# Gate matmuls moved behind the weighted sums, and the context limit to the front of VectorE's list, in a pass-pipelined attention and expert kernel

## The reference

```python
logits = x @ gate_weight.T                       # 8 experts
topk_w, topk_idx = jax.lax.top_k(softmax(logits), 2)
y = routed experts (silu(gate) * up, down) + shared expert
x = x + y
```

## Time and profile before

| What | Value |
|---|---|
| median of three runs | 1449.7 us (1448.55 to 1450.1) |
| the profiled execution | 1446.31 us, its span 1444.6 us |
| mean granted TensorE clock | 0.98 |
| TensorE busy | 1340.1 us, 93% of the span |
| VectorE, ScalarE, GpSimd busy | 61%, 47%, 26% |
| chain that ended last, by engine | TensorE 80%, VectorE 11%, issue 2%, ScalarE 2%, DMA 2% |

### The profile page before, as it was taken

How to read it: one execution, slowest core, us unless ns; L and a number is a source line. 1 busy time by engine, 2 the same in 40 slices (tenths; PEclk the granted TensorE clock), 3 DMA queues, 4 the chain that set the end, 5 groups by cost and what they waited for, 6 DMA issues and landing times.

```text
span 1444.6 us, 34230 instructions
## 1 busy us (share of the span) xinstructions
PE 1340.1 (93%) x11411; PEld 1005.0 (70%) x11412; DVE 884.4 (61%) x1952; ACT 674.4 (47%) x1500; POOL 372.7 (26%) x480
## 2 busy tenths in 40 slices
PE   4799999999999997788999999999999999999997
PEld 4688788888888885656767756666666666657675
DVE  6888888888888888667855532232232232224566
ACT  6276667777676776431444423333333333332121
POOL 4322222222222220004566011111111111104554
PEclk9899999999999998899999999999999999999999
DMA  5556766776767658497734622222222222227996
GB/s 197 134 141 190 198 196 185 204 204 199 189 185 202 185 138 270 129 350 134 113 53 83 148 95 81 80 86 80 81 85 82 80 86 81 81 72 235 315 312 225
DMA packets 212740, 223.20 MB, mean 155 GB/s; under 512 B 84693, under 2 KB 142109, under 8 KB 212334
## 3 DMA queue, kind: packets, MB, share of 16 engines
q1 hardware_dynamic: 193608, 178.62, 43.5%
q0 software_dynamic: 12880, 35.47, 8.1%
q10 hardware_dynamic: 6198, 8.40, 2.0%
HBM read 129.30 MB, written 67.96 MB: 137 GB/s over the span
## 4 chain that ended last, share of the span: by engine, by line
PE 80%; DVE 11%; issue 2%; ACT 2%; DMA 2%; SPq 1%; POOL 0%; DVEq 0%; POOLq 0%; ACTq 0%
PE psum_b L726 44%; PE psum_a L726 30%; PE psum_b L1016 2%; PE psum_b L1038 2%; DVE z_parts L1472 1%; DVE k_scale L1394 1%; DVE d_m L1705 1%; PE psum_b L752 1%; SPq L488 1%; DVE wdn L1791 1%; DMA heads<-in_wk_t 1%; DVE gate_act L1680 1%; ACT z_parts L1120 1%; DMA wgu_in<-base_rows 1%; PE psum_b L784 0%
## 5 line engine op out<-in xcount | busy, mean ns | idle before, releaser
L726 PE MATMUL psum_a<-wgu,zg_t 128*128 x1704 | 267.7, 314 | 2.1 <-DVE zg_t L1802 1.7
L726 PEld LDWEIGHTS psum_a<-wgu,zg_t 128*128 128x128 f16 x1704 | 166.1, 98 | 90.2 <-issue 10.3
L726 PE MATMUL psum_a<-zt_in,wsgu 128*128 128x256 f16 x1536 | 170.6, 273 | 1.0 <-ACT y_sb L1306 0.8
L2025 POOL DMA_INDIRECT zg<-z_rows,gather_ix x71 | 67.2, 946 | 402.9 <-DVE gather_ix L1798 395.8
L726 PEld LDWEIGHTS psum_a<-zt_in,wsgu 128*128 128x128 f16 x1536 | 148.8, 98 | 24.9 <-issue 6.5
L1807 DVE SCALAR_TENSOR_TENSOR silu<-psum_a,w_scale,silu 128x352 f32<-128x352 f32 x71 | 41.5, 584 | 191.1 <-ACT silu L1293 191.1
L726 PE MATMUL psum_b<-wdn,act_t 128*128 (+1 forms) x639 | 149.6, 379 | 1.6 <-DVE act_t L1814 1.6
L726 PE MATMUL psum_b<-wsdn,sh_t 128*128 128x512 f16 (+1 forms) x576 | 134.4, 388 | 14.9 <-DVE sh_t L1686 14.4
L1912 POOL TENSOR_SCALAR var_eps<-mv 128x1 f32<-128x1 f32 x64 | 28.4, 443 | 429.7 <-DVE mv L1371 289.9
L1293 ACT ACTIVATE silu<-psum_a,w_scale 128x352 f32<-128x352 f32 x71 | 39.4, 554 | 202.4 <-PE psum_a L726 202.4
L726 PEld LDWEIGHTS psum_b<-wsdn,sh_t 128*128 128x128 f16 (+1 forms) x576 | 54.6, 99 | 88.9 <-issue 18.3
(11 more groups left out here) (247 smaller groups left out, 2346.8 us busy)
## 6 DMA issues: line engine op xcount, KB each, us to landing
expert_rows<-y_sb SPq DMA_DIRECT2D x71, 256.0 KB, 2.0
k_st<-k_parts SPq DMA_DIRECT2D x192, 64.0 KB, 2.0
q_st<-q_parts SPq DMA_DIRECT2D x180, 64.0 KB, 2.0
wgu_in<-in_wgu_t SPq DMA_DIRECT2D x8, 1408.0 KB, 16.5
x_sb<-in_x SPq DMA_DIRECT2D x16, 512.0 KB, 5.5
cx_in<-in_ctx_t SPq DMA_DIRECT2D x16, 512.0 KB, 8.8
x_res<-in_x SPq DMA_DIRECT2D x16, 512.0 KB, 6.3
value_rows<-heads SPq DMA_DIRECT2D x16, 512.0 KB, 3.3
```

The source lines that it names most:

```text
L726: return nc.tensor.matmul(o, l, r, start=start, stop=stop)
L2025: pool.indirect_dma_start(out=zg[:, b, :], out_offset=None, in_=z_d[:, :], in_offset=bass.IndirectOffsetOnAxis(ap=gather_ix[:, b:b + 1], a ...
```

## The change

The gate matmuls of a pass get a step of their own, R, in bank A0 (that of the first scores), instead of L in B2; only pass 16, outside the loop, keeps L in B2. On TensorE the weighted sums come directly behind turning z, then the gate matmuls, then `turn_bound`, then `turn_logits`, which now also waits until R is drained. ScalarE copies both halves of z ahead of the two high halves. VectorE finds and spreads the context's limit right behind the values, ahead of `z_low` and `logits_out`.

```diff
-ROUTE = [("L", "B2")]
+ROUTE = [("R", "A0")]
+LAST_ROUTE = [("L", "B2")]
...
-FULL_PASS = (AHEAD + SCORES + AHEAD_KQ + OUT + AHEAD_V + BEHIND + ROUTE
-             + [("P0", "A2"), ("P1", "A3")] + TURN_ROUTE + BOUND)
+FULL_PASS = (AHEAD + SCORES + AHEAD_KQ + OUT + AHEAD_V + BEHIND + ROUTE + LAST_ROUTE
+             + [("P0", "A2"), ("P1", "A3")] + BOUND + TURN_ROUTE)
...
+def route_step(i):
+    return "L" if isinstance(i, int) and i == NB else "R"
...
             def route(i):
-                wait_free(pe, "L", i)
+                wait_free(pe, route_step(i), i)
...
             def turn_logits(i):
                 wait_free(pe, "LT", i)
+                settle(pe)
+                wait_drained(pe, route_step(i), i)
                 settle(pe)
...
                 if behind:
                     turn_z(i)
-                if behind:
-                    route(i)
                 attend(0, i)
                 attend(1, i)
                 if behind:
-                    turn_logits(i)
+                    route(i)
                 if ahead:
                     turn_bound(i)
+                if behind:
+                    turn_logits(i)
...
             def z_out(i):
                 turned_out(i, 0)
+                turned_out(i, 1)
                 z_high(i, 0)
-                turned_out(i, 1)
...
                 if ahead:
                     values_out(i)
+                if ahead2:
+                    weigh_context(i + 2)
+                if ahead:
+                    spread_context()
                 if behind:
                     z_low(i, 0)
                     logits_out(i)
                     z_low(i, 1)
-                if ahead2:
-                    weigh_context(i + 2)
-                if ahead:
-                    spread_context()
                 if weighs:
                     weigh_piece(i, weighs)
```

More of the change, by code:

```diff
@@ L86 @@
 IS_BEHIND = {name for name, _ in OUT + BEHIND + ROUTE + TURN_ROUTE}
+ONLY_LAST = {name for name, _ in LAST_ROUTE}
 def steps_of(i):
     names = [name for name, _ in FULL_PASS]
+    if i == NB:
+        return [n for n in names if n in IS_BEHIND - {"R"} | ONLY_LAST]
+    names = [name for name in names if name not in ONLY_LAST]
     if i < 0:
         return [n for n in names if n in IS_AHEAD]
-    if i == NB:
-        return [n for n in names if n in IS_BEHIND]
     return [n for n in names if not (i == 0 and n in IS_BEHIND) and not (i == NB - 1 and n in IS_AHEAD)]
@@ L105, in earlier_fills @@
         return whole + sum(n in mine for n in names[:names.index(step)])
-    return (i - 1) * len(mine) + earlier_fills(step, 1)
+    return (i - 1) * len(mine - ONLY_LAST) + earlier_fills(step, 1)
+def route_step(i):
+    return "L" if isinstance(i, int) and i == NB else "R"
 class Chain:
@@ L787, in route @@
             def route(i):
-                wait_free(pe, "L", i)
+                wait_free(pe, route_step(i), i)
                 pe.wait_ge(z_turned, i * SUB)
                 for kc in range(KC):
-                    last = mm(bank_ap("L")[HD * kc:HD * (kc + 1), 0:BT], wgate[:, kc, :], z_t[:, kc, :], True, True)
-                last.then_inc(full[BANK_OF["L"]], 1)
+                    last = mm(bank_ap(route_step(i))[HD * kc:HD * (kc + 1), 0:BT], wgate[:, kc, :], z_t[:, kc, :], True, True)
+                last.then_inc(full[BANK_OF[route_step(i)]], 1)
             def turn_logits(i):
                 wait_free(pe, "LT", i)
+                settle(pe)
+                wait_drained(pe, route_step(i), i)
                 settle(pe)
@@ L1476, in logits_out @@
             def logits_out(i):
-                wait_full(dve, "L", i)
-                V.tensor_copy(logits_t[:, :], bank_ap("L")[:, 0:BT]).then_inc(drained[BANK_OF["L"]], 1)
+                wait_full(dve, route_step(i), i)
+                V.tensor_copy(logits_t[:, :], bank_ap(route_step(i))[:, 0:BT]).then_inc(drained[BANK_OF[route_step(i)]], 1)
             def turned_logits_out(i):
```

## The result

| | before | after |
|---|---|---|
| median of four runs each, on one chip | 1449.9 us (1448.55 to 1454.31) | **1471.8 us** (1469.05 to 1472.4) |
| profiled execution, its span | 1446.3, 1444.6 | 1472.3, 1470.6 |
| turning x of pass 1 starts | 81.58 | 82.34 |
| turning x of pass 14 starts | 523.95 | 542.31 |
| sums of pass 15 start | 584.96 | 604.65 |

The ratio is **1.0142, with a 95% interval of 1.0109 to 1.0175**: slower, by over three times what was forecast. The lower rows of the table are read downwards, as differences of the two kernels: +0.76, +18.36, +19.69, +24.32, +26.08, +25.6. Behind the first down matmul nothing is lost any more. So 17.6 us arose in passes 1 to 13 (460.0 for 442.4 us), 7.7 at the end of the attention, 0.8 ahead of pass 1.

What follows compares the result with a forecast made beforehand. VectorE, not TensorE, was taken to set most of the 6.65 us between turning z and the keys. Steady passes 0, pass 15 5.1 and clock 1.8 gave 6.9 us more: median 1449.7 to 1456.6, range 1449.2 to 1460.5.

Steps and rivals of the forecast that it cites:

- The copy is held: VectorE's copy spreading the limit over c_rep, passes 1 to 13: about 1.8 us, until GpSimd's subtraction ends; before, 0.23.
- the rule that the prediction drew: VectorE's two-port copy and a GpSimd instruction exclude each other; tensor_reduce never contends: early maximum free, copy held.
- The sum: Steady pass, VectorE's queue up to M0, the limit's transpose: 317.61 + 0.60 + 0.34 + 0.69 + 0.12 = 319.36.
- The step from M0 to turning x: Steady pass, turned logits now between: 0.83 us, the middle of bounds 0.60 and 1.06.
- the term of 0: Steady passes 1 to 13: keys start at 321.28 against 321.30, so nothing gained.
- 9.21 us from the sums to the shared gate matmuls: Pass 15: logits copy and shared weights wait behind the sums, shared gate matmuls at 594.51, 5.1 us later.
- 1.8 us for their clock: Pass 15: TensorE idles 3.4 us, its clock falls, costing 1.8 us; bounds 0 and 2.4.
- the 0.34: Pass 14: Z1's low half, column store and loads behind it 0.34 us later, delaying pass 15's sums to 585.30.
- the term for steady passes: Passes 1 to 13: 0; bounds 0.25 gained or 0.21 lost per pass, 3.2 or 2.7 us over 13.
- Rivals 2 and 3: 2: attention's end pays little, 1451.4 us, chance 0.13. 3: SyncE falls behind, 0.3 us per pass, 1460.5 us, chance 0.05.
- Rival 1: Passes 1 to 13: c_rep copy not held, 1.00 us less per pass, 1443.6 us; chance 0.12.

Runs made afterwards that it cites:

- e2: Changed kernel with GpSimd's subtraction in the context split made to wait for VectorE's copy of the limit; 1458.8 us, ratio 1.0012 to the kernel before.
- e4: Changed kernel with the last two shared weights of pass 15 ahead of the logits copy on VectorE; 1472.9 us, ratio 1.0099 to the kernel before.
- e1: Changed kernel with eight filler matmuls into unread bank A1 behind the gate matmuls of passes 1 to 14; 1458.1 us, ratio 1.0019 to the kernel before.
- f1: Changed kernel with GpSimd's wait, five filler matmuls, and pass 15's last two shared weights ahead of the logits copy; 1431.3 us, ratio 0.9879 to the kernel before.
- f2: Changed kernel with GpSimd's subtraction behind the limit's copy and five filler matmuls, pass 15 as changed; 1440.4 us, ratio 0.9949 to the kernel before.
- e3: Changed kernel with the turned logits again ahead of the context limit's transpose M0 on TensorE; 1463.8 us, ratio 1.0039 to the kernel before.
- e8: f1 without the filler matmuls, with the turned logits ahead of the limit's transpose M0; 1435.3 us, ratio 0.9879 to the kernel before.
- e6: Kernel before with only VectorE's new order, the limit behind the values; ratio 1.0262, 38.1 us above the kernel before.

## Why the prediction was wrong, step by step

**Right.** The copy is held until GpSimd's subtraction ends: predicted about 1.8 us, measured 1.93 here and 0.23 in e2, where it is kept apart. With the rule that the prediction drew from the Trainium skill, "SBUF — State Buffer", section "Who interferes with whom", the runs agree as far as they go: the maximum beside GpSimd kept its 1.21 us, the copy did not keep its 0.23. In which mode the copy ran, on which the rule depends, no run shows. The sum went on from 317.61, the end of the subtraction, and not from 317.68, where it had put the end of the copy; measured, Z0's low half started 0.01 us behind the subtraction (328.07 and 328.06), so that was the right choice. M0 starts 4.64 us behind the turned z (predicted 4.71), released by Z1's low half. The step from M0 to turning x is 1.01 us for my 0.83, near the upper bound, 1.06, which was worked out for a loop's jump that hides behind nothing. A pass at full clock is 34.05 to 34.12 us, so the term of 0 was right for the instructions.

In pass 15 the forecast was 9.21 us from the sums to the shared gate matmuls and 1.8 us for their clock; measured 9.11 and 1.76 (31.59 for 29.83 us to the first down matmul). The sums start 1.33 us later from pass 14 on where I had 0.34, for pass 14 too begins at a fallen clock. Together 7.7 for 6.9. e4 confirms the mechanism. Whether the 0.34 was right stays open: where pass 14 began at full clock, the sums of pass 15 came 60.6 to 61.0 us behind its turning x in e1, f1 and f2 and 61.6 in e3, for 61.0 before.

**The step that failed** is the term for steady passes, "nothing gained. The bounds are 0.25 gained or 0.21 lost per pass". I compared the starts of instructions, 321.28 with 321.30, and let each run at the length it had before. My own sum had TensorE stand still from 317.2 to 319.4, where before the idle time lay in three pieces between matmuls; in pass 15 I priced just that, a clock that falls when TensorE runs dry, and did not ask it of the other 13. The term measured 17.6 us, where its bounds were 3.2 gained and 2.7 lost, and e1 takes away all of it (19.3 with its shorter full-clock pass). With the 0.8 us more at the end of the attention and the 0.8 ahead of pass 1 that is the whole miss: the profiled execution took 1472.3 us for 1453.2. Rivals 2 and 3 did not occur. Rival 1's pass, 1.0 us shorter, came true in e2 and f1 (1.3 shorter, at full clock) once GpSimd was ordered, so its working was right in direction and its condition, a copy that nothing holds, did not hold in this kernel.

**Open.** What exactly holds the clock. Fillers, 512 columns wide, in the stretch between turning z and the keys kept it in all 39 passes of e1, f1 and f2. The same stretch holds only narrow or short matmuls otherwise (32-column weights, 8-column results, single transposes), in the kernel before too, and there it kept the clock with 2.29 us of idle, while e8 lost it with 0.89. One difference that remains is the order, since the kernel before has its longest idle time ahead of gate matmuls and sums and e8 behind them; but e6, with 3.76 us at that same early place, lost the clock as well. Neither the length of the idle time nor its place alone tells the outcome, and this was not settled. Nor was it tested whether the fillers must be wide: no run filled the wait with narrow matmuls. The nearest pair speaks for it without showing it: e1 still idled 0.16 and 0.49 us around its fillers and kept the clock in 13 passes, e8 idled 0.64 and 0.25 us and lost it in 8.

## What to carry to other kernels

When a change moves TensorE's idle time, price the clock as well as the starts, in every repetition of the loop, and where a wait must stay, try a few matmuls into an unused bank in it: five of 512 columns, with nothing else changed in a pass (f2 against e2), kept 2.4 GHz here and cost no time, a pass at full clock being 32.7 us with and without them. When VectorE's work is moved, look at what GpSimd does at the new place; one semaphore between two operations of 0.23 and 2.36 us took away a stall of 1.7. And look at what else stands in the queue behind a moved wait in the last, unrolled pass.

## What the runs showed of the hardware

The granted clock fell to 1.2 GHz behind a stretch of narrow matmuls with no idle time above 0.64 us (e8), and stayed at 2.4 GHz with one of 1.54 us in another order; two ends of a pass with the same rows differed in it, so it must be read per pass and never from one. In e2 turning x began at full clock in seven passes in a row and was caught midway, each time a little earlier: it took 1.28, 1.36, 1.45, 1.56, 1.69, 1.79 and 1.88 us. The seven falls (147.71 to 352.51) came 34.13 us apart and the passes took 34.2 to 34.3, so turning x moved on against the falls by 0.1 us a pass: the moment of a fall did not keep to one place among the pass's instructions. And a pass that lost its clock was stretched from 32.5 or so to 34.1 us in e8 and then kept losing it, six times in a row, with the falls again 34.13 us apart (148.59 to 319.25), until it broke off.

GpSimd's 128x1024 subtraction held VectorE's 128x128 copy beside it until its own end: 1.93 us for 0.23 in the kernel after, 1.83 in e6, and 0.23 again in e2, f1 and f2, where the two were kept apart.
